# Relative values of a decoder's third self-attention: one product per query with its exps as the stationary operand

## The chip, the cores and the metric

The kernel runs on one core of one Trainium2 chip. The metric is the device time of one execution of the whole program, in microseconds (us); the kernel before was timed three times. TensorE (PE in the profile, PEld for its weight loads) multiplies, VectorE (DVE), ScalarE (ACT) and GpSimd (POOL) do the element-wise work, SyncE (SP) issues DMAs. A matrix product has a stationary operand, which is loaded into the array first (LDWEIGHTS), and a moving operand, which streams through it (MATMUL). In float32 the profile holds two LDWEIGHTS and two MATMUL records for each product, and one of each for a transpose.

## The reference

The model has four decoder layers of self-attention, cross-attention and feed-forward, twelve blocks in all, on x of shape (8, 128, 128). The change lies in the third layer's self-attention alone:

```python
def _L2_attn_ref(hidden_states, Wq, bq, Wk, bk, Wv, bv, Wo, bo, rel_k_emb, rel_v_emb):
    B, T, E = hidden_states.shape          # 8, 128, 128; H = 16 heads of D = 8
    ...                                    # qh, kh, vh: (B, H, T, D)
    score1 = jnp.einsum('bhqd,bhkd->bhqk', qh, kh)
    rel_k = _rel_embeds(rel_k_emb, T, T)   # table[q - k + 128], (T, T, D)
    s2 = jnp.einsum('bhqd,qkd->qbhk', qh, rel_k) ...
    attn = jax.nn.softmax((score1 + s2) / scaling, axis=-1)
    w1 = jnp.einsum('bhqk,bhkd->bhqd', attn, vh)
    rel_v = _rel_embeds(rel_v_emb, T, T)   # (q, k, d)
    se = attn.reshape(B * H, T, T).transpose(1, 0, 2)
    w2 = jnp.einsum('qnk,qkd->qnd', se, rel_v)      # the part that the change rewrites
    ...
    return (w1 + w2) ... @ Wo.T + bo
```

For w2 each query q has a matrix of its own, rel_v[q] (128 keys by 8), that is multiplied with the attention rows of all 128 pairs of a head and a batch.

## The kernel before

Each block is one function; the blocks run one after another with a barrier between them, and within a block each engine's instructions stand in program order and wait for each other by semaphores. `layer_l2_attn` first makes queries, keys and values, then the relative scores of the keys (L2446 to L2464), then runs sixteen pipelined steps of scores, exp, values and norm (L2473 to L2494). The exps of all heads and batches stay in `sm.prob`, 128 keys on the partitions by (16 heads times 8 batches) by 128 queries, so that the 128 exps of one query and one key lie 128 elements apart. The ordinary values, divided by the sum of exps, are in `sm.o`.

After the steps comes what the change touches:

- **Products** (L2496 to L2505). For every query, `relv[:, q, :]` (128 keys by 8 values and a column of ones) is stationary, 9 columns wide, and the query's exps move, 32 at a time in four products, each into its own group of 32 output partitions. That is 512 products. The results of 16 queries fill one PSUM bank; eight banks are filled.
- **Copies** (L2550 to L2554 on ACT, L2588 to L2592 on DVE). Each bank is copied to `oR` as it comes, ACT and DVE by turns. `oR` lies over `qm`, which is no longer needed.
- **Tail.** PE waits for the last copies (L2508 to L2510), then for each batch turns four 128x128 blocks back so that queries are on the partitions (L2512). DVE takes the reciprocal of the ones' column (L2598) and multiplies (L2603), POOL adds the result to `sm.o` (L2424), PE turns the sum (L540), ACT copies it out (L620), PE multiplies it with the output weights (L545), and DVE adds it to x (L596). A batch's turns, norm, sum, turn and projection are software-pipelined over the ten passes of `for step in range(B + 2)`; `part` has two halves, so the multiply of batch b waits for the sum of batch b - 2.

The next block is `layer_l2_xattn` (its first PE work is L664, L667 and the transposes L445). Three other places serve for comparison: L888 and L1143 are the routers' logits (tokens 128x128 stationary, 8 columns moving), L764 makes joined weights in the next layer's self-attention (128x128 stationary, 32 or 16 columns moving), and L3573 is a convolution whose stationary operand has 8 columns that lie 128 elements apart.

Of the kernel before, what the change touches and what calls it, by code (L numbers as in the profile page):

```python
# [12 lines left out]
ALU = mybir.AluOpType  # L13
# [11 lines left out]
P = 128  # L25

B = 8
# [7 lines left out]
BANK = 512  # L35
# [2345 lines left out]
def layer_l2_attn(core, tag, w):  # L2381

    nc, ps, norm = core.nc, core.ps, NormInBlock(core)
    c = Carve(core.scratch)
    wq, wk, wv, wo, of_four, bq, bk = w.take(P), w.take(P), w.take(P), w.take(D), w.take(4), w.take(4), w.take(1)
    bq1, bv, bo, relk, relv = w.take(1), w.take(D), w.take(D), w.take(2 * P), w.take(P, 9)
    qm = w.take(4, B * P)
    sm = RelativeHeads(core, c, wo, more=Carve(core.xnT), o=w.take(B * 16, 8))  # L2390
    oR = qm.rearrange("p i t -> p (i t)").rearrange("p (b j t) -> p b j t", b=B, j=4)
    part, part_inv = w.take(2 * 16, 8).rearrange("p (u h) d -> p u h d", u=2), w.take(2, 16)
    made_of = sm.prob.rearrange("p (b j i) q -> p j b i q", b=B, j=4)
    read_by = sm.prob.rearrange("p (y s m z) q -> p y z s m q", y=2, s=8, z=2)
    keys = core.xn[:, :, :].rearrange("p b d -> p (b d)")
    TURN = 16
    ROUNDS = P // TURN
# [8 lines left out]
    with nc.Block(tag, no_gpsimd_drain=True) as block:  # L2406

        @block.gpsimd
        def _(pool):
# [12 lines left out]
            for b in range(B):  # L2422
                pool.wait_ge(relv_normed.sem, relv_normed.at(b))
                nc.gpsimd.tensor_tensor(sm.o_of(b), sm.o_of(b), part[:, b % 2, :, :], ALU.add) \  # L2424
                    .then_inc(relv_summed.sem, relv_summed.up())

        @block.tensor
        def _(pe):
# [7 lines left out]
            for b in range(B):  # L2436
                v = nc.tensor.matmul(ps[2 + b // 4][:, b % 4 * P:(b % 4 + 1) * P], core.xnT[:, b * P:(b + 1) * P],
                                     wv, start=True, stop=True)
# [7 lines left out]
            for r in range(ROUNDS):  # L2446
# [8 lines left out]
                for t in range(TURN):  # L2455
                    q = r * TURN + t
# [16 lines left out]
            for p in range(-2, sm.STEPS + 2):  # L2473
# [11 lines left out]
                if p % 2 and p >= 3:  # L2485
                    b = (p - 3) // 2
# [9 lines left out]
            for r in range(ROUNDS):  # L2496
                if r == 7:
                    pe.wait_ge(sm.normed.sem, sm.normed.at(B - 1))
                for t in range(TURN):
                    q = r * TURN + t  # L2500
                    for i in range(4):
                        m = nc.tensor.matmul(
                            ps[r][32 * i:32 * i + 9, 32 * t:32 * t + 32].rearrange("p (b j) -> p b j", b=B),
                            relv[:, q, :], read_by[:, i % 2, i // 2, :, :, q], start=True, stop=True)
                m.then_inc(relv_made.sem, relv_made.up())  # L2505
            for step in range(B + 2):
                if step < B:
                    if step == 0:  # L2508
                        pe.wait_ge(relv_act.sem, relv_act.at(3))
                        pe.wait_ge(relv_dve.sem, relv_dve.at(3))  # L2510
                    for j in range(4):
                        t = nc.tensor.transpose(ps[step][:, j * P:(j + 1) * P], oR[:, step, j, :], core.ident[:, :])  # L2512
                    t.then_inc(relv_back.sem, relv_back.up())
                if 1 <= step <= B:
                    pe.wait_ge(relv_summed.sem, relv_summed.at(step - 1))
                    sm.pe_turn_out(pe, step - 1, step - 1)
                if step >= 2:
                    sm.pe_project(pe, step - 2, step - 2)

        @block.scalar  # L2520
        def _(act):
# [28 lines left out]
            for r in range(0, ROUNDS, 2):  # L2550
                act.wait_ge(relv_made.sem, relv_made.at(r))
                nc.scalar.copy(oR[:, :, :, r * TURN:(r + 1) * TURN],
                               ps[r][:, :].rearrange("p (t b j) -> p b j t", t=TURN, b=B)) \
                    .then_inc(relv_act.sem, relv_act.up())  # L2554
# [4 lines left out]
        def _(dve):  # L2559
# [28 lines left out]
            for r in range(1, ROUNDS, 2):  # L2588
                dve.wait_ge(relv_made.sem, relv_made.at(r))
                nc.vector.tensor_copy(oR[:, :, :, r * TURN:(r + 1) * TURN],  # L2590
                                      ps[r][:, :].rearrange("p (t b j) -> p b j t", t=TURN, b=B)) \
                    .then_inc(relv_dve.sem, relv_dve.up())  # L2592
            for step in range(B + 2):
                if step < B:
                    b = step
                    dve.wait_ge(relv_back.sem, relv_back.at(b))
                    o = ps[b][:, :].rearrange("p (h d) -> p h d", d=32)
                    nc.vector.reciprocal(part_inv[:, b % 2, :], o[:, :, 8]) \  # L2598
                        .then_inc(relv_inverse.sem, relv_inverse.up())
                    dve.wait_ge(relv_inverse.sem, relv_inverse.at(b))  # L2600
                    if b >= 2:
                        dve.wait_ge(relv_summed.sem, relv_summed.at(b - 2))
                    nc.vector.tensor_tensor(part[:, b % 2, :, :], o[:, :, 0:8],  # L2603
                                            part_inv[:, b % 2, :].unsqueeze(2).broadcast_to([P, 16, 8]), ALU.mult) \
                        .then_inc(relv_normed.sem, relv_normed.up())
                if step == 2:
                    dve.wait_ge(x_biased.sem, x_biased.at(0))
                if step >= 2:
                    sm.dve_add(dve, step - 2, step - 2)
# [1355 lines left out]
```

## Time and profile before

| | us |
|---|---|
| runs: median (lowest to highest of 3) | 1424.65 (1420.49 to 1427.03) |
| the profiled execution | 1414.56 |
| its span, first to last instruction | 1412.7 |
| PE busy | 1227.3 (87% of the span) |
| the changed block's products, start of the first to start of the last | 928.7 to 957.0 |
| the tail, to the next block's first instruction | to 969.1 |

The profiled execution lasts 1.9 us longer than its span and lies 10.1 us below the median of the three runs. A window row gives each engine's busy time in a stretch and PEclk, the granted TensorE clock: 1.00 is 2.4 GHz, 0.50 is 1.2 GHz.

### The profile page before, as it was taken

The page shows a single profiled execution, that of the slowest core. Times are in us where ns is not written, and L with a number is a line of the kernel's source. Part 1 is how long each engine was busy: PE and PEld are TensorE (multiplying, and loading weights), DVE is VectorE, ACT ScalarE, POOL GpSimd, SP SyncE. Part 2 cuts the span into 40 slices and gives each one's busy share as a digit, 9 for nine tenths or more (in the row PEclk, how much of TensorE's full clock was granted, in tenths as well). Part 3 has the DMA queues.
Part 4 walks back from the last instruction along what each step waited for, and adds up shares of the span by engine and source line. Part 5 has one row for each costly group of instructions (what it writes and reads, how often), then busy time and mean ns, then how long its engine had stood idle before and what let it go on. Part 6 is the DMA issues. An engine that isn't in the chain of part 4 may idle for free. (4 is left out here: it accounts for less than half of the span.)

```text
span 1412.7 us, 25671 instructions
## 1 busy us (share of the span) xinstructions
PE 1227.3 (87%) x10296; PEld 905.8 (64%) x10296; DVE 685.4 (49%) x2133; ACT 515.5 (36%) x1170; POOL 437.2 (31%) x519
## 2 busy tenths in 40 slices
PE   6999697999878756987898899998989999977897
PEld 5868585788623433664665697795657775565575
DVE  5555533444489154774674315626842125745312
ACT  5534242443356322454354212213433323433231
POOL 7969220000245326754672400003000001041404
PEclk9999798999956678999899658999989997989899
DMA  5000402321290000000000000000021100001312
GB/s 159 1 4 1 188 7 90 91 61 47 95 255 1 1 10 23 1 1 0 2 1 1 9 2 1 2 4 1 2 82 45 31 29 1 1 4 37 121 29 46
DMA packets 51639, 52.51 MB, mean 37 GB/s; under 512 B 19553, under 2 KB 42337, under 8 KB 50497
## 3 DMA queue, kind: packets, MB, share of 16 engines
q1 hardware_dynamic: 50496, 48.77, 11.0%
q0 software_dynamic: 1024, 2.10, 0.7%
q8 instruction: 83, 1.36, 0.4%
q14 instruction: 36, 0.29, 0.1%
HBM read 43.65 MB, written 7.21 MB: 36 GB/s over the span
## 5 line engine op out<-in xcount | busy, mean ns | idle before, releaser
L615 ACT ACTIVATE scratch<-bank 128x512 f32<-128x512 f32 x96 | 52.4, 594 | 88.9 <-PE bank L516 88.9
L574 DVE TENSOR_REDUCE scratch<-bank 128x4 f32<-128x512 f32 x96 | 63.2, 686 | 35.4 <-PE bank L2469 22.4
L439 POOL TENSOR_TENSOR ln_rstd<-ln_ve,ln_half 128x4 f32<-128x4 f32 x28 | 28.7, 1025 | 155.7 <-DVE ln_ve L418 155.5
L2721 POOL TENSOR_TENSOR scratch<-scratch 128x16 f32<-128x16 f32 x16 | 51.7, 3231 | 51.8 <-DVE scratch L3062 51.8
L1085 PEld LDWEIGHTS bank<-scratch 128*128 128x128 f32 x512 | 59.5, 192 | 7.2 <-issue 7.2
L1114 ACT ACTIVATE scratch<-bank 128x512 f32<-128x512 f32 x64 | 38.2, 597 | 67.4 <-PE bank L1075 67.4
L580 DVE TENSOR_TENSOR scratch<-bank,scratch 128x512 f32<-128x512 f32 x96 | 61.4, 681 | 0.0
L1133 DVE SCALAR_TENSOR_TENSOR x_res<-bank,scratch,x_res 128x128 f32<-128x128 f32 x64 | 18.0, 344 | 87.6 <-PE bank L1085 87.6
L1075 PE MATMUL bank<-xnT,scratch 128*128 128x512 f32 x128 | 59.6, 611 | 0.0
L1085 PE MATMUL bank<-scratch 128*128 128x128 f32 x512 | 59.6, 275 | 0.0
L516 PEld LDWEIGHTS bank<-ident,scratch 128*128 128x128 f32 x384 | 42.7, 143 | 23.7 <-DVE scratch L580 17.0
L516 PE MATMUL bank<-ident,scratch 128*128 128x128 f32 x384 | 53.6, 283 | 4.7 <-DVE scratch L580 4.7
L2459 PE MATMUL bank<-weights 32*128 32x32 f32 x1024 | 54.7, 395 | 2.5 <-DVE scratch L2573 2.5
L2459 PEld LDWEIGHTS bank<-weights 32*128 32x128 f32 x1024 | 54.6, 327 | 3.3 <-issue 3.3
L500 PE MATMUL bank<-scratch 32*128 32x512 f32 x192 | 54.0, 643 | 1.4 <-ACT scratch L2542 1.4
L1293 PE MATMUL bank<-scratch 128*128 128x128 f32 (+1 forms) x352 | 47.0, 291 | 9.0 <-issue 8.9
L1293 PEld LDWEIGHTS bank<-scratch 128*128 128x128 f32 (+1 forms) x352 | 45.0, 201 | 13.5 <-issue 12.5
L2750 PE MATMUL bank<-weights,xnT 128*128 128x512 f32 x64 | 39.5, 714 | 14.8 <-DVE scratch L3032 14.2
L2424 POOL TENSOR_TENSOR weights<-weights 128x128 f32<-128x128 f32 x8 | 3.7, 458 | 154.0 <-DVE weights L2603 154.0
L1887 POOL TENSOR_TENSOR x_res<-x_res,scratch 128x256 f32<-128x256 f32 x4 | 2.9, 726 | 143.6 <-ACT scratch L2031 143.6
L1358 ACT ACTIVATE scratch<-bank 128x512 f32<-128x512 f32 (+1 forms) x48 | 25.4, 544 | 57.8 <-remote 27.5
L3264 POOL TENSOR_TENSOR scratch<-scratch 128x1024 f32<-128x1024 f32 (+5 forms) x48 | 42.9, 895 | 3.8
(564 smaller groups left out, 3023.7 us busy)
## 6 DMA issues: line engine op xcount, KB each, us to landing
scratch<-conv_kernels SPq DMA_DIRECT2D x8, 1024.0 KB, 11.2
scratch<-e_l_ffn_w SPq DMA_DIRECT2D x20, 256.0 KB, 2.9
scratch<-e_l_ffn_w SPq DMA_DIRECT2D x4, 1024.0 KB, 14.8
values<-scratch SPq DMA_DIRECT2D x8, 512.0 KB, 2.6
scratch<-values SPq DMA_DIRECT2D x8, 512.0 KB, 4.3
weights<-w_l_ffn SPq DMA_DIRECT2D x1, 3698.0 KB, 11.6
scratch<-e_l_ffn_w SPq DMA_DIRECT2D x4, 768.0 KB, 9.5
weights<-w_l_attn SPq DMA_DIRECT2D x1, 2560.5 KB, 8.8
```

The costliest lines, as they stand in the source:

```text
L500: s = self.nc.tensor.matmul(self.by_head(self.core.ps[n % 4][:, :]), self.qT[rows, b * P:(b + 1) * P], self.km[rows, :, b * P:(b + 1) * P] ...
L516: t = self.nc.tensor.transpose(self.core.ps[4 + n % 2][:, i * P:(i + 1) * P], self.shift[:, n % 4, i * P:(i + 1) * P], self.core.ident[:, :])
L574: self.nc.vector.tensor_reduce(self.top[:, n % 4, :], self.by_head(self.core.ps[n % 4][:, :]), AX_X, ALU.max, negate=True).then_inc(self.t ...
L580: self.nc.vector.tensor_tensor(self.by_head(self.shift[:, n % 4, :]), self.by_head(self.core.ps[n % 4][:, :]), self.top[:, n % 4, :].unsqu ...
L615: self.nc.scalar.activation(self.prob_of(n), self.by_head(self.core.ps[4 + n % 2][:, :]), ACT.Exp, scale=scale) \
L1075: nc.tensor.matmul(ps[UP_BANKS[i]][:, :], wa[e % 2][:, i * P:(i + 1) * P], core.xnT[:, half(h)], start=True, stop=True).then_inc(up_made.s ...
L1085: mm = nc.tensor.matmul(ps[Y_BANKS[u % 3]][:, t * P:(t + 1) * P], hT[h][:, i, t * P:(t + 1) * P], wb[e % 2][:, i, :], start=(i == 0), stop ...
L1293: mm = nc.tensor.matmul(ps[Y_BANKS[j % 3]][0:n, t:t + P], hT[j % 2][:, i, t:t + n], wb[:, e, i, :], start=(i == 0), stop=(i == HC - 1))
L2459: m = nc.tensor.matmul(ps[4 * (r % 2) + j][:, 32 * t:32 * t + 32].rearrange("p (i b) -> p i b", i=4), relk[rows, P - 1 - q:2 * P - 1 - q], ...
L2721: nc.gpsimd.tensor_tensor(rn, ss, power, ALU.pow).then_inc(rooted.sem, rooted.up())
L2750: nc.tensor.matmul(ps[QK_BANKS[n]][:, :], core.xnT[:, b * P:(b + 1) * P], wqkv[d][:, n * BANK:(n + 1) * BANK], start=True, stop=True).then ...
L3264: link(tt(out, prod[:, :, 0:h], prod[:, :, h:2 * h], ALU.add))
```

## The change

The operands of the relative values swap their places: for each query all 128 exps become the stationary operand and `relv[:, q, :]` with its 9 columns moves. The result of a query is 9 columns wide with (head, batch) on all 128 partitions. 56 queries fit a bank, so three banks hold them (56, 56 and 16 queries), and three copies instead of eight put them into `oR`, now nine planes of 128 queries. Nine transposes bring back the plane of ones and the eight planes of values, for all batches at once; one reciprocal and four multiplies of 256 columns norm them; POOL adds batch by batch as before, now from strided views.

```diff
-    oR = qm.rearrange("p i t -> p (i t)").rearrange("p (b j t) -> p b j t", b=B, j=4)
-    part, part_inv = w.take(2 * 16, 8).rearrange("p (u h) d -> p u h d", u=2), w.take(2, 16)
+    over_queries = Carve(qm.rearrange("p i t -> p (i t)"))
+    oR, part, part_inv = over_queries.take(9, P), over_queries.take(8, 2, P // 2), over_queries.take(2, P // 2)
+    HELD = BANK // 9 // 2 * 2
+    HELDS = [slice(n, min(n + HELD, P)) for n in range(0, P, HELD)]
+    ONES_BANK, PART_BANKS = len(HELDS), (len(HELDS) + 1, len(HELDS) + 2)
+    held = lambda r: (oR[:, :, HELDS[r]].rearrange("p d q -> p q d"),
+                      ps[r][:, 0:9 * (HELDS[r].stop - HELDS[r].start)].rearrange("p (q d) -> p q d", d=9))
...
 (POOL)
-                pool.wait_ge(relv_normed.sem, relv_normed.at(b))
-                nc.gpsimd.tensor_tensor(sm.o_of(b), sm.o_of(b), part[:, b % 2, :, :], ALU.add) \
+                pool.wait_ge(relv_normed.sem, relv_normed.at(2 * (b // 4) + 1))
+                o = sm.o_of(b).rearrange("p (m y) d -> p d y m", y=2)
+                nc.gpsimd.tensor_tensor(o, o, part[:, :, :, 8 * b:8 * b + 8], ALU.add) \
...
 (PE)
-            for r in range(ROUNDS):
-                if r == 7:
-                    pe.wait_ge(sm.normed.sem, sm.normed.at(B - 1))
-                for t in range(TURN):
-                    q = r * TURN + t
-                    for i in range(4):
-                        m = nc.tensor.matmul(
-                            ps[r][32 * i:32 * i + 9, 32 * t:32 * t + 32].rearrange("p (b j) -> p b j", b=B),
-                            relv[:, q, :], read_by[:, i % 2, i // 2, :, :, q], start=True, stop=True)
+            for r, queries in enumerate(HELDS):
+                for q in range(queries.start, queries.stop):
+                    t = q - queries.start
+                    m = nc.tensor.matmul(ps[r][:, 9 * t:9 * t + 9], sm.prob[:, :, q], relv[:, q, :], start=True, stop=True)
                 m.then_inc(relv_made.sem, relv_made.up())
-            for step in range(B + 2):
+            pe.wait_ge(relv_dve.sem, relv_dve.at(0))
+            pe.wait_ge(relv_act.sem, relv_act.at(1))
+            nc.tensor.transpose(ps[ONES_BANK][:, 0:P], oR[:, 8, :], core.ident[:, :]) \
+                .then_inc(relv_back.sem, relv_back.up())
+            for n in range(2):
+                for d in range(4):
+                    t = nc.tensor.transpose(ps[PART_BANKS[n]][:, d * P:(d + 1) * P], oR[:, 4 * n + d, :], core.ident[:, :])
+                t.then_inc(relv_back.sem, relv_back.up())
+            for step in range(B + 1):
                 if step < B:
-                    if step == 0:
-                        pe.wait_ge(relv_act.sem, relv_act.at(3))
-                        pe.wait_ge(relv_dve.sem, relv_dve.at(3))
-                    for j in range(4):
-                        t = nc.tensor.transpose(ps[step][:, j * P:(j + 1) * P], oR[:, step, j, :], core.ident[:, :])
-                    t.then_inc(relv_back.sem, relv_back.up())
-                if 1 <= step <= B:
-                    pe.wait_ge(relv_summed.sem, relv_summed.at(step - 1))
-                    sm.pe_turn_out(pe, step - 1, step - 1)
-                if step >= 2:
-                    sm.pe_project(pe, step - 2, step - 2)
+                    pe.wait_ge(relv_summed.sem, relv_summed.at(step))
+                    sm.pe_turn_out(pe, step, step)
+                if step >= 1:
+                    sm.pe_project(pe, step - 1, step - 1)
...
 (ACT)
-            for r in range(0, ROUNDS, 2):
+            for r in (0, 2):
                 act.wait_ge(relv_made.sem, relv_made.at(r))
-                nc.scalar.copy(oR[:, :, :, r * TURN:(r + 1) * TURN],
...
+                nc.scalar.copy(*held(r)).then_inc(relv_act.sem, relv_act.up())
...
 (DVE)
+            dve.wait_ge(relv_made.sem, relv_made.at(1))
+            nc.vector.tensor_copy(*held(1)).then_inc(relv_dve.sem, relv_dve.up())
+            dve.wait_ge(relv_back.sem, relv_back.at(0))
+            nc.vector.reciprocal(part_inv, ps[ONES_BANK][:, 0:P].rearrange("p (y c) -> p y c", y=2)) \
+                .then_inc(relv_inverse.sem, relv_inverse.up())
+            dve.wait_ge(relv_inverse.sem, relv_inverse.at(0))
+            for h in range(2):
+                batches = slice(32 * h, 32 * h + 32)
+                for n in range(2):
+                    dve.wait_ge(relv_back.sem, relv_back.at(1 + n))
+                    nc.vector.tensor_tensor(
+                        part[:, 4 * n:4 * n + 4, :, batches],
+                        ps[PART_BANKS[n]][:, :].rearrange("p (d y c) -> p d y c", d=4, y=2)[:, :, :, batches],
+                        part_inv[:, :, batches].unsqueeze(1).broadcast_to([P, 4, 2, 32]), ALU.mult) \
+                        .then_inc(relv_normed.sem, relv_normed.up())
+            dve.wait_ge(x_biased.sem, x_biased.at(0))
+            for b in range(B):
+                sm.dve_add(dve, b, b)
```

On PE, from the end of the sixteen steps to the next block, there stood before (output by its name, operands, shape as output partitions by columns; `L540` is a batch's turn, `L545` its projection):

```order
L535 MATMUL bank<-ident,xnT 128x128 x4
L2502 MATMUL bank<-scratch,weights 9x32 x512
L2512 MATMUL bank<-ident,weights 128x128 x8
L540 MATMUL bank<-ident,weights 128x128
L2512 MATMUL bank<-ident,weights 128x128 x4
L540 MATMUL bank<-ident,weights 128x128
L545 MATMUL bank<-weights,xnT 128x128
L2512 MATMUL bank<-ident,weights 128x128 x4
L540 MATMUL bank<-ident,weights 128x128
L545 MATMUL bank<-weights,xnT 128x128
```

In the changed kernel (its line numbers are those of its own file) the same place reads:

```order
L535 MATMUL bank<-ident,xnT 128x128 x4
L2507 MATMUL bank<-weights,scratch 128x9 x128
L2511 MATMUL bank<-ident,weights 128x128
L2515 MATMUL bank<-ident,weights 128x128 x8
L540 MATMUL bank<-ident,weights 128x128 x2
L545 MATMUL bank<-weights,xnT 128x128
L540 MATMUL bank<-ident,weights 128x128
L545 MATMUL bank<-weights,xnT 128x128
```

The 512 products became 128 of another shape, and the turns back, which stood in fours between a batch's turn and projection, all stand ahead of the first batch.

On DVE, over the same stretch, there stood before (reciprocal, multiply, and from the third batch on the add to x):

```order
L2590 COPY weights<-bank 128x32x16 x4
L2598 RECIPROCAL weights<-bank 128x16
L2603 TENSOR_TENSOR weights<-bank,weights 128x128
L2598 RECIPROCAL weights<-bank 128x16
L2603 TENSOR_TENSOR weights<-bank,weights 128x128
L2598 RECIPROCAL weights<-bank 128x16
L2603 TENSOR_TENSOR weights<-bank,weights 128x128
L596 TENSOR_TENSOR x_res<-x_res,bank 128x128
```

Now the norm is done in five instructions before the first add:

```order
L2591 COPY weights<-bank 128x56x9
L2593 RECIPROCAL weights<-bank 128x128
L2600 TENSOR_TENSOR weights<-bank,weights 128x8x32 x4
L596 TENSOR_TENSOR x_res<-x_res,bank 128x128 x8
```

What moved is the norm: DVE's sixteen small instructions, spread over the batches, are five ahead of them.

## Rows read from the trace of the kernel before

**Rows 1.** The page: the span, and PE's and PEld's busy time.
```profile
span 1412.7 us, 25671 instructions
PE 1227.3 (87%) x10296; PEld 905.8 (64%) x10296; DVE 685.4 (49%) x2133; ACT 515.5 (36%) x1170; POOL 437.2 (31%) x519
```

**Rows 2.** Windows (start:end, length; PE, PEld, DVE, ACT, POOL busy; PEclk; DMA): products, tail.
```profile
928.70:957.20 28.50, 28.43 (x1025) 27.97 (x1024) 3.00 (x5) 2.35 (x4) 0.00 (x0) 1.00 0.02 5
957.20:969.10 11.90, 8.06 (x61) 6.23 (x56) 7.01 (x25) 2.13 (x8) 3.66 (x8) 1.00 0.00 0
```

**Rows 3.** One line's instructions, L888: count, ns min/median/max.
```profile
L888 PEld LDWEIGHTS bank<-weights,xnT x32: 286/333/333, 1039.6 to 1310.2; 128*128 128x128 f32 x32
L888 PE MATMUL bank<-weights,xnT x32: 351/361/361, 1039.6 to 1310.3; 128*128 128x8 f32 x32
```

**Rows 4.** Timeline of PE (start, duration us, operation, count): other stretches.
```profile
1039.60 3.55 PE L888 MATMUL bank<-weights,xnT 128*128 128x8 f32 x16 [0.88 <-DVE xnT L1122]
...
794.49 0.91 PE L2459 MATMUL bank<-weights 32*128 32x32 f32 x16 [2.51 <-DVE scratch L2573]
...
1159.04 3.20 PE L764 MATMUL bank<-weights 128*128 128x32 f32 x18 [1.56 <-PEq L1045]
...
1150.18 7.31 PE L1085 MATMUL bank<-scratch 128*128 128x128 f32 x64
...
852.61 3.73 PE L2469 MATMUL bank<-ident,scratch 128*128 128x128 f32 x16
857.33 2.05 PE L2469 MATMUL bank<-ident,scratch 128*128 128x128 f32 x16
```

**Rows 5.** Windows around L2459 and L764, columns as in rows 2.
```profile
794.50:794.90 0.40, 0.40 (x12) 0.40 (x13) 0.00 (x0) 0.40 (x1) 0.00 (x0) 0.78 0.00 0
794.90:848.00 53.10, 53.10 (x1003) 53.10 (x1001) 9.02 (x14) 8.22 (x16) 14.33 (x9) 0.50 0.01 2
850.60:856.00 5.40, 5.40 (x20) 3.90 (x20) 0.69 (x1) 0.00 (x0) 0.00 (x0) 0.50 0.00 0
1159.00:1159.90 0.90, 0.86 (x8) 0.89 (x9) 0.86 (x5) 0.90 (x1) 0.32 (x1) 1.00 0.00 0
1160.50:1168.20 7.70, 7.70 (x38) 7.70 (x38) 3.25 (x17) 0.74 (x2) 2.02 (x2) 0.50 0.14 52
```

**Rows 6.** Narrow weights, 128 elements apart (L3573) and side by side (L527).
```profile
L3573 PEld LDWEIGHTS bank<-scratch x256: 91/97/133, 480.3 to 493.2; 128*8 128x8 f32 x128
...
L527 PEld LDWEIGHTS bank<-scratch x768: 86/91/92, 867.0 to 1242.8; 128*9 128x9 f32 x192
```

**Rows 7.** Timeline of the tail.
```profile
957.33 0.69 DVE L2590 COPY weights<-bank 128x512 f32<-128x512 f32 x1 [6.48 <-PE bank L2502]
...
958.16 1.06 PE L2512 MATMUL bank<-ident,weights 128*128 128x128 f32 x8 [0.88 <-DVE weights L2590]
...
959.49 0.95 POOL L2424 TENSOR_TENSOR weights<-weights 128x128 f32<-128x128 f32 x2 [149.97 <-DVE weights L2603]
...
967.25 0.33 PE L540 MATMUL bank<-ident,weights 128*128 128x128 f32 x1 [0.30 <-POOL weights L2424]
...
968.46 0.29 DVE L596 TENSOR_TENSOR x_res<-x_res,bank 128x128 f32<-128x128 f32 x1 [0.33 <-PE bank L545]
```

**Rows 8.** Groups by line and form: busy us, mean ns, idle before.
```profile
L620 ACT COPY xnT<-bank 128x128 f32<-128x128 f32 x8 | 2.1, 266 | 11.6 <-PE bank L540 11.6
...
L3044 DVE TENSOR_TENSOR scratch<-bank,scratch 128x256 f32<-128x256 f32 x32 | 12.0, 416 | 0.0
...
L2424 POOL TENSOR_TENSOR weights<-weights 128x128 f32<-128x128 f32 x8 | 3.7, 458 | 154.0 <-DVE weights L2603 154.0
...
L1887 POOL TENSOR_TENSOR x_res<-x_res,scratch 128x256 f32<-128x256 f32 x4 | 2.9, 726 | 143.6 <-ACT scratch L2031 143.6
```

**Rows 9.** Timeline: the next block's first PE work.
```profile
969.14 1.95 PE L664 MATMUL bank<-ctxT_sb,weights 96*128 96x512 f32 x4 [0.72 <-PEq L2406]
...
970.93 1.95 PE L667 MATMUL bank<-weights,ctxT_sb 96*128 96x128 f32 x16
```

More of the change, by code:

```diff
@@ L2390, in layer_l2_attn @@
     sm = RelativeHeads(core, c, wo, more=Carve(core.xnT), o=w.take(B * 16, 8))
-    oR = qm.rearrange("p i t -> p (i t)").rearrange("p (b j t) -> p b j t", b=B, j=4)
-    part, part_inv = w.take(2 * 16, 8).rearrange("p (u h) d -> p u h d", u=2), w.take(2, 16)
+    over_queries = Carve(qm.rearrange("p i t -> p (i t)"))
[5 more added lines that the diff above has]
+                      ps[r][:, 0:9 * (HELDS[r].stop - HELDS[r].start)].rearrange("p (q d) -> p q d", d=9))
     made_of = sm.prob.rearrange("p (b j i) q -> p j b i q", b=B, j=4)
-    read_by = sm.prob.rearrange("p (y s m z) q -> p y z s m q", y=2, s=8, z=2)
     keys = core.xn[:, :, :].rearrange("p b d -> p (b d)")
@@ L2549, in _ @@
                     sm.act_outs(act, p // 2 - 1)
-            for r in range(0, ROUNDS, 2):
+            for r in (0, 2):
                 act.wait_ge(relv_made.sem, relv_made.at(r))
-                nc.scalar.copy(oR[:, :, :, r * TURN:(r + 1) * TURN],
-                               ps[r][:, :].rearrange("p (t b j) -> p b j t", t=TURN, b=B)) \
-                    .then_inc(relv_act.sem, relv_act.up())
+                nc.scalar.copy(*held(r)).then_inc(relv_act.sem, relv_act.up())
             for b in range(B):
@@ L2587, in _ @@
                     sm.dve_norm(dve, (p - 4) // 2, 7)
[L2588 to L2604, printed above, removed]
+            dve.wait_ge(relv_made.sem, relv_made.at(1))
@@ L2605, in _ @@
                         .then_inc(relv_normed.sem, relv_normed.up())
[L2606 to L2609, printed above, removed]
+            dve.wait_ge(x_biased.sem, x_biased.at(0))
+            for b in range(B):
+                sm.dve_add(dve, b, b)
 def layer_l1_ffn(core, tag, w):
```

## The prediction

> **What bounds the kernel now.** I read four views, in this order. The page says that PE is busy for 87% of the span [rows 1], so I expect a stage's time to be set on PE. A table by windows of the changed stretch confirms it: in the products' 28.5 us PE is busy for 28.43 at the high clock, with DVE busy for 3.0 and ACT for 2.35, so the copies hide completely; in the 11.9 us of the tail PE is busy for 8.06, DVE for 7.01 and POOL for 3.66, so there the chain from engine to engine sets the time and nobody is full [rows 2]. The products have 1024 records, so one costs 28.5 / 1024 = 27.8 ns. The third view is other lines whose operation looks like the new one, and the last is the granted clock around them. The reader should see that the question is not how many instructions there are, but what one of the new kind costs, and at which clock.
>
> **The products.** Removed: 512 products, 1024 records, 28.5 us. Added: 128 products, 256 records, each with a 128x128 weight load and 9 moving columns. That shape nearly stands in the trace: L888 loads 128x128 and moves 8 columns. Its 16 records take 3.55 us in all and one lasts 0.361 [rows 3, 4], so they start (3.55 - 0.36) / 15 = 0.213 us apart, at the 1.2 GHz clock. A matmul of 128 moving columns behind the same load runs at the high clock with 64 records in 7.31 us, (7.31 - 0.28) / 63 = 0.112 us apart [rows 4]. So the moving operand hardly matters and the weight load sets the pace: 0.213 us at the low clock, 0.107 to 0.112 at the high one. For 256 records that is 54.5 us or 27.3 to 28.6 us. At the high clock the change would win at most 1.2 us here, although it issues a quarter of the instructions, since each now loads 128 columns instead of 9.
>
> The granted clock then decides. Two stretches of the trace had a wide weight load for few moving columns and went on for long: L2459 (128 columns loaded, 32 moving) and L764 (128x128 loaded, 32 or 16 moving). Both began at the high clock, in both it fell to 1.2 GHz, and it stayed there for 53.1 us and 7.7 us, although PE shows busy for every one of those microseconds [rows 5]. Dense work brought it back only after about 5 us: at 0.50 from 850.6 to 856.0 [rows 5]. The new product moves 9 columns for 128 loaded, less than either, for 128 products in a row. I therefore take the low clock for the whole stage but its start. How long the start is: L2459 was reached after 2.51 us of idle and lost the clock 0.4 us later, L764 after 1.56 us and lost it after more than 0.9 us [rows 4, 5]. That is 2.9 and 2.5 us after the last dense record; I take 2.7 us, bounds 0 and 6. In 2.7 us at 0.107 come 25 records; the other 231 take 231 x 0.213 = 49.2 us. Stage: 51.9 us, and the last record ends 0.36 after its start where it was 0.27 or so, +0.1. **Products: 51.9 + 0.1 - 28.5 = +23.5 us**, bounds +20 and +26.
>
> Here two rules of the Trainium skill have a say. "TensorE: Matmul & The Clock Gate", section "What's actually happening", says that activity releases the throttle, the clock following how busy the engine has been. Read by the profile's busy share it would keep the clock high, and the sum would be that of the first rival. Rows 5 contradict that reading, since PE is 100% busy there at 1.2 GHz.
>
> The other is the note on cachelines in "SBUF — State Buffer", section "Door 1: The DMA port swizzle": each access that crosses to a new 16-byte line pays a penalty. By that rule the strided weight loads would be dearer than L888's contiguous ones, and the sum would be the second rival's. The trace agrees only to a small part, as the following shows.
>
> The new weights are read 128 elements apart. L3573 loads 8 such columns in 91/97/133 ns (min/median/max), L527 loads 9 adjacent ones in 86/91/92 [rows 6]. The medians differ by 6 ns over 8 columns; scaled to 128 it is 96 ns on a record, as an upper bound. The minima differ by 5 ns, which may as well be fixed. Bounds per record: 0 and +0.1 us at the high clock, so up to twice the price; I take 0, because at the low clock, where the stage will be, nothing of it shows: the full contiguous load of L888 lasts 333 ns and the slowest strided one of 8 columns 133, and (333 - 133) / 120 = 1.67 ns a column is just L888's own pace, 213 / 128 [rows 3, 6].
>
> **The copies.** Three in place of eight. Two of them finish under the products. The last holds 16 queries x 9 = 144 columns on ACT; the nearest row is 0.27 us for 128 columns [rows 8], so 0.28 for a copy of 0.69 that stood on the path [rows 7]. The gain is 0.4 us. A written stride of 128 elements has no row of its own; bounds 0.28 and 0.6.
>
> **The tail.** Before: the last product ends at about 957.3, the last add to x at 968.46 + 0.29 = 968.75 [rows 7], which is 11.45 us. I build the new one from T, the last product's end. The copy runs from T + 0.05 to T + 0.33; PE starts 0.14 later as before (957.33 + 0.69 to 958.16 [rows 7]), at T + 0.47. At the low clock transposes start (3.73 - 0.42) / 15 = 0.22 us apart, at the high one (2.05 - 0.27) / 15 = 0.12 [rows 4]. The clock is still low here. The fifth transpose ends at T + 0.47 + 4 x 0.22 + 0.42 = T + 1.8, the ninth at T + 2.65. The reciprocal hides under them; the multiplies of 256 columns cost 0.42 each [rows 8]; the first finishes at T + 2.2, the second at T + 3.1, and POOL starts at T + 3.2. Batches 0 to 3 need no more than these two; the other two multiplies (to T + 4.0) are ready before POOL reaches batch 4 at T + 5.1.
>
> POOL makes eight adds 0.475 us apart (0.95 for two [rows 7]), up to T + 7.0. Its views are strided now; for that I have no row, the nearest being 0.458 for the same 128 columns and 0.726 for twice as many [rows 8], so bounds of 0 and +2.1 us, and I take 0. PE needs for a batch a turn and two projection records, 3 x 0.22 = 0.65 us at the low clock and 0.36 at the high one. So at first PE sets the pace, and once the clock is back POOL does. Dense records of rows 5 needed 5 us for that, so about half of the eight batches run at either pace: 0.6 us more, T + 7.6. The last batch's turn, copy, projection and add took 968.75 - 967.25 = 1.5 us [rows 7]. End at T + 9.1, which is 2.3 us less than 11.45. **Tail: -2.3 us.** Bounds: all warm, T + 0.47 + 0.7 + 0.3 (five transposes, the rest of the ninth under the multiplies), POOL from T + 1.8, end at T + 7.1, which is -4.3; PE at its low pace throughout and POOL at its dear end, T + 11, which is -0.4. What is late next is POOL at the high clock and PE at the low one. The first batch's turn and projection, which started 2 us after T, now wait for the norm of all; that is in the sum.
>
> **The next block.** L664 and L667 take 3.7 us at the high clock [rows 9]. If the low clock reached them they would take up to 3.7 more. I think it comes back within the tail, which has 9 transposes and 24 further records; I take +1.0, bounds 0 and +3.7.
>
> **Sum.** 23.5 - 2.3 + 1.0 = +22.2 us. The rest of the program is the same instructions in the same order. Against the profiled execution of 1414.56 us (its span 1412.7 [rows 1] and 1.9 around it) this gives 1436.8. That execution is 10.1 us below the median of the runs, 1424.65, so for the measured time I add the difference to the median: 1424.65 + 22.2 = 1446.9, **1447 us**.
>
> **Rivals.**
>
> - *The clock stays at 2.4 GHz* (the other side). The stage starts from a long dense stretch instead of after idle time, which neither L2459 nor L764 did. Then the products cost 27.3 to 28.6 and save 0.6 on average, and the tail saves 4.3: -4.9 us, 1420. It decides from a clock that is high for over 25 us of the 27. Against it: the clock did not return in 53 us of L2459. Chance 0.06.
> - *The strided weight load costs double.* 512 cycles in place of 256, 0.427 us a record at the low clock: 231 x 0.213 = 49 us more, with a slightly shorter gain at the start, 1496. For it: the 6 ns of rows 6 and the page. Chance 0.06; milder forms of it (10% dearer, +5 us) belong to the range of the main case.
> - *The clock comes and goes* within the stage, low for half of it: products +11, tail -3, 1433. For it: in rows 5 the clock was high for the first 0.4 and 0.9 us of such work. Against: it never came back before dense work did. Chance 0.06.
>
> **Chances.** Forecast 0.82, its own range 1438 to 1457 (products ±3, tail ±2, next block -1 to +2.7, and the runs' own spread, 1420.5 to 1427). What a measurement can tell from no change is 0.5%, 7.1 us. The first rival lies inside it, mostly: faster 0.02, same 0.05 (with a little of the third). Everything else is slower: 0.93. Range 1436 to 1458: the three rivals and the edges of the forecast leave about 0.2 outside.
>
> **What would show it.** PEclk 0.5 in the window of the new products from their third microsecond on, weight loads of 0.333 us starting 0.213 apart, a stage of 52 us; transposes of the tail 0.22 apart; POOL's eight adds following each other with DVE already done. Wrong would be: a stage near 28 us at PEclk 1.0 (first rival); weight loads well over 0.333 us (second); PEclk between 0.6 and 0.9 over the stage (third); POOL adds over 0.6 us each would make the tail no shorter.

## The result, and the profile after

| | before | changed | ratio, 95% interval |
|---|---|---|---|
| median of the first comparison (4 runs each) | 1422.57 | 1450.20 | 1.0197 [1.0166, 1.0227] |
| median of a later one (16 and 5 runs) | 1422.06 | 1448.61 | 1.0188 [1.0164, 1.0212] |
| profiled execution | 1414.56 | 1449.16 | |

The changed kernel is slower by 27 us: 27.6 in the first comparison, 26.6 in the later one. The forecast of 1447 us lies 3 us from the measured 1450.20. As the experiments show, one of the reasons given for it was not what set the pace.

The products, read from the windows of the changed kernel's own product line (start:end, length, PE and PEld busy with records in the window, PEclk, DMA):

```profile
931.70:935.10 3.40, 3.40 (x17) 3.40 (x17) 1.00 0.00 0
935.20:986.90 51.70, 51.70 (x240) 51.70 (x239) 0.50 0.00 1
```

These answer to the first row of [rows 2]. The clock fell as forecast, 3.5 us into the stage, and stayed down. But the records tell something else: 17 in 3.40 us is one every 0.20 to 0.21 (one of them belongs to the window's edge), 240 in 51.7 is one every 0.215, and over the whole stage it is 55.3 / 255 = 0.217. **The pace is the same at both clocks.** The forecast's sum had 0.107 for the first part and 0.213 for the second. The line's own instructions (count, ns min/median/max, first and last start) say it in another way:

```profile
L2507 PEld LDWEIGHTS bank<-weights,scratch x256: 295/310/313, 931.6 to 986.9; 128*128 128x128 f32 x128
L2507 PE MATMUL bank<-weights,scratch x256: 281/366/371, 931.7 to 987.0; 128*128 128x9 f32 x128
```

A weight load lasts 295 to 313 ns throughout, in the first 3.4 us at the high clock as well as later. L888's, of the same size, adjacent and mostly at the low clock, lasts 333 [rows 3]. In a run told below, with adjacent weights and the clock high throughout, the same load lasts 190 to 192:

```profile
L2509 PEld LDWEIGHTS bank<-weights,scratch x256: 190/192/192, 928.5 to 957.0; 128*128 128x128 f32 x128
```

None of the changed kernel's loads is that short. The stage goes from 931.7 to 987.0 + 0.37 = 987.3, 55.7 us in place of 28.6.

The tail, as a timeline (start, duration, what it waited for), answers to [rows 7]:

```profile
987.37 0.40 ACT L2556 COPY weights<-bank 128x144 f32<-128x144 f32 x1 [30.25 <-PE bank L2507]
...
987.91 0.45 PE L2511 MATMUL bank<-ident,weights 128*128 128x128 f32 x1 [0.58 <-ACT weights L2556]
...
988.15 1.91 PE L2515 MATMUL bank<-ident,weights 128*128 128x128 f32 x8
988.40 0.96 DVE L2593 RECIPROCAL weights<-bank 128x128 f32<-128x128 f32 x1 [6.96 <-PE bank L2511]
989.39 0.42 DVE L2600 TENSOR_TENSOR weights<-bank,weights 128x256 f32<-128x256 f32 x1
990.10 1.09 DVE L2600 TENSOR_TENSOR weights<-bank,weights 128x256 f32<-128x256 f32 x3 [0.29 <-PE bank L2515]
990.61 4.08 POOL L2432 TENSOR_TENSOR weights<-weights 128x128 f32<-128x128 f32 x8 [177.94 <-DVE weights L2600]
...
991.21 0.98 PE L540 MATMUL bank<-ident,weights 128*128 128x128 f32 x2 [1.15 <-POOL weights L2432]
...
996.00 0.42 PE L540 MATMUL bank<-ident,weights 128*128 128x128 f32 x1
...
996.87 0.73 DVE L596 TENSOR_TENSOR x_res<-x_res,bank 128x128 f32<-128x128 f32 x2 [0.33 <-PE bank L545]
...
997.99 1.95 PE L664 MATMUL bank<-ctxT_sb,weights 96*128 96x512 f32 x4 [0.72 <-PEq L2413]
```

It ends at 997.6, 10.3 us after the products, where it was 11.45. POOL's eight adds take 4.08 us in a row and are done at 994.7. PE's eight turns, each followed by its projection, start 0.68 us apart (991.21 to 996.00), with the granted clock at 0.50 up to 996. So it is PE at the low clock that sets this part, and POOL is ahead of it. The next block starts with products of 1.95 us for four records, as in [rows 9]: the low clock did not reach it. From the start of the products to the next block's first product it is 66.3 us (931.68 to 997.99) where it was 40.5 (928.67 to 969.14): **+25.8 us**.

The two spans differ by 34.6. Some 3.0 us lie before the changed stage. They do not belong to the change: over all profiles of this case the stage starts between 923.7 and 934.3 us, and in the changed kernel's second profile it starts at 927.1, ahead of both profiles of the kernel before (928.7 and 929.5). The other 5.8 lie behind it, in the next block, which took 76.6 us up to the routers' products (998.0 to 1074.6) where it had taken 70.5; the rest of the program took 0.3 less. In the changed kernel the clock fell in it:

```profile
998.00:1010.30 12.30, 10.40 (x54) 5.88 (x56) 9.29 (x34) 5.92 (x12) 6.35 (x6) 1.00 0.01 0
1010.30:1023.90 13.60, 13.60 (x73) 7.12 (x70) 8.82 (x15) 3.76 (x7) 2.19 (x2) 0.50 0.00 1
```

PEclk is the third number from the end. The experiments tell whether that belongs to the change.

### The profile page after: what moved, and what is told of

It reads as the page before. It is cut to its first block and busy times, and to the rows that moved or that the text cites. A ratio compares the mean times of both kernels' runs of the same rounds, so it can differ in the third digit from the quotient of the medians.

```text
span 1447.3 us, 24068 instructions
## 1 busy us (share of the span) xinstructions
PE 1264.5 (87%) x9505; PEld 938.6 (65%) x9505; DVE 682.2 (47%) x2119; ACT 515.1 (36%) x1168; POOL 438.3 (30%) x519
## 3 DMA queue, kind: packets, MB, share of 16 engines
q1 hardware_dynamic: 50496, 48.77, 10.7%
## 5 line engine op out<-in xcount | busy, mean ns | idle before, releaser
L439 POOL TENSOR_TENSOR ln_rstd<-ln_ve,ln_half 128x4 f32<-128x4 f32 x28 | 28.7, 1026 | 162.8 <-DVE ln_ve L418 162.7
L2719 POOL TENSOR_TENSOR scratch<-scratch 128x16 f32<-128x16 f32 x16 | 51.7, 3232 | 50.9 <-DVE scratch L3060 50.9
L500 PE MATMUL bank<-scratch 32*128 32x512 f32 x192 | 57.3, 679 | 1.4 <-ACT scratch L2546 1.4
L2507 PEld LDWEIGHTS bank<-weights,scratch 128*128 128x128 f32 x256 | 55.7, 310 | 0.0
L2507 PE MATMUL bank<-weights,scratch 128*128 128x9 f32 x256 | 55.7, 366 | 0.0
```

The costliest lines, as they stand in the source:

```text
L500: s = self.nc.tensor.matmul(self.by_head(self.core.ps[n % 4][:, :]), self.qT[rows, b * P:(b + 1) * P], self.km[rows, :, b * P:(b + 1) * P] ...
L2507: m = nc.tensor.matmul(ps[r][:, 9 * t:9 * t + 9], sm.prob[:, :, q], relv[:, q, :], start=True, stop=True)
L2719: nc.gpsimd.tensor_tensor(rn, ss, power, ALU.pow).then_inc(rooted.sem, rooted.up())
```

## The experiments

Two theories stood against each other. **A:** a weight load whose elements lie 128 apart has a pace of its own, 0.217 us a record, whatever the clock. **B**, which the forecast's sum used: the pace is that of an adjacent load and only the granted clock matters. The first three runs and the changed kernel form a square: weights strided or adjacent, 9 or 128 columns moving.

### Adjacent weights, 9 columns moving

```diff
-  m = nc.tensor.matmul(ps[r][:, 9 * t:9 * t + 9], sm.prob[:, :, q], relv[:, q, :], start=True, stop=True)
+  m = nc.tensor.matmul(ps[r][:, 9 * t:9 * t + 9], sm.prob[:, q, :], relv[:, q, :], start=True, stop=True)
```

> The changed kernel, but each product's stationary operand is 128 adjacent elements of the exps (another query's set, so the values are not the reference's) instead of 128 elements that lie 128 apart. 9 columns move as in the changed kernel. Theory A (a strided weight load sets the pace, 0.217 us a record at either clock): as long as the clock is high, in the first 3 us or so, records start 0.107 us apart instead of 0.217; once it has fallen, 0.213. Stage 50 to 53 us, time about 3 us below the changed kernel. Theory B (only the granted clock sets the pace, as I predicted): 0.217 apart in the first microseconds too, stage 55.7 as in the changed kernel, no change.

Measured: 1444.85 us, ratio 1.0155 [1.0117, 1.0193]. Windows of the product line:

```profile
930.80:933.90 3.10, 3.10 (x29) 3.10 (x29) 1.00 0.00 0
934.00:982.00 48.00, 48.00 (x227) 48.00 (x227) 0.50 0.00 1
```

29 records in 3.10 us at the high clock, 0.107 to 0.112 each; 227 in 48.0 at the low one, 0.21 each. Stage 51.7 us, and the time is 4 to 5 us below the changed kernel's 1448.61 and 1450.20, where about 3 were expected. The forecast had 51.9 for the stage: its sum describes this kernel with adjacent weights, not the changed one. Theory A stands: with the stride gone the pace follows the clock.

### Strided weights, 128 columns moving

```diff
+  wide = min(P, 9 * (P - q))
-  m = nc.tensor.matmul(ps[r][:, 9 * t:9 * t + 9], sm.prob[:, :, q], relv[:, q, :], start=True, stop=True)
+  m = nc.tensor.matmul(ps[r][:, 9 * t:9 * t + wide], sm.prob[:, :, q], relv_flat[:, 9 * q:9 * q + wide], ...)
```

> The changed kernel with its strided weights, but 128 columns of the relative values move behind each load instead of 9; of the result only the 9 are kept (the next product writes over the rest). 40 queries fill a bank instead of 56, so there are four copies instead of three. I expect the granted clock to be 1.00 in the stage. Theory A (strided weights set the pace at either clock): records stay 0.217 us apart, stage 54 to 56 us, and only the tail and the next block gain, by 2 to 8 us in all. Theory B (the clock sets the pace): 0.11 us apart, stage about 28 us, time 25 to 32 us below the changed kernel.

Measured: 1448.98 us, ratio 1.0184 [1.0146, 1.0221].

```profile
933.80:987.90 54.10, 54.10 (x248) 54.10 (x248) 1.00 0.00 1
```

The clock is at 2.4 GHz for 54 us, and a record still takes 54.1 / 248 = 0.218. Theory B falls. The 2 to 8 us expected from tail and next block did not come: in the profiled run, the slowest of its four (1453.75 us), the clock fell at the last, narrower products, PEclk was 0.59 on average in the tail, and from the products' end to the next block it took 10.3 us, where the changed kernel took 10.7.

### Adjacent weights, 128 columns moving

Both edits together.

> Both edits together: the weights are 128 adjacent elements (another query's set, so the values are not the reference's) and 128 columns move. Both theories expect the high clock and records 0.107 to 0.115 us apart, a stage of 27 to 30 us and a time within 0.5% of the kernel before. If the stage stays near 55 us, neither the stride nor the clock is what costs.

Measured: 1419.45 us, ratio 0.9988 [0.9961, 1.0016], no difference from the kernel before.

```profile
928.70:957.00 28.30, 28.30 (x255) 28.30 (x255) 1.00 0.00 1
```

28.3 / 255 = 0.111 us a record. Only with both costs gone does the stage return to 28.6 us. In a table, us a record and us a stage:

| | 9 columns move | 128 columns move |
|---|---|---|
| weights 128 apart | 0.217, 55.7 (changed kernel; clock low) | 0.218, 56.1 (clock high) |
| weights adjacent | 0.213, 51.7 (clock low) | 0.111, 28.7 (clock high) |

Each cause alone costs nearly everything; together they cost hardly more. They do not add: the strided load has its 0.217 at either clock, and the adjacent load at the low clock happens to have almost the same pace, 0.213. The tail of this run, 957.3 to the next block at 966.8, takes 9.5 us with the clock partly high, 2.4 less than before.

### How far apart may weights lie

The kernel with 128 moving columns, whose weights lie 2 elements apart for the first 40 queries, then 4, then 3, and 128 for the last 8:

```diff
+  HELD, STEPS_OF = 40, (2, 4, 3, 128)
-  ... sm.prob[:, :, q], ...
+  ... sm.prob.rearrange("p n q -> p (n q)")[:, q:q + (P - 1) * STEPS_OF[r] + 1:STEPS_OF[r]], ...
```

> As the kernel with 128 moving columns (clock high), but the 128 weights of a product lie 2 elements apart for the first 40 queries, 4 apart for the next 40, 3 apart for the next 40 and 128 apart for the last 8 (other exps than the reference's, so the values are not the reference's). Theory A1 (what costs is that each 16-byte line is used for one element only): 0.112 us a record for 2 apart, 0.217 for 4 and for 128, and in between or 0.217 for 3. Theory A2 (any step but 1 costs): 0.217 in all four parts. Theory A3 (only large steps cost): 0.112 for 2, 3 and 4, 0.217 for 128.

One run, 1433.57 us. One window inside each part:

```profile
924.00:933.00 9.00, 9.00 (x78) 9.00 (x77) 1.00 0.01 2
934.00:951.00 17.00, 17.00 (x75) 17.00 (x74) 1.00 0.00 0
953.00:965.00 12.00, 12.00 (x71) 12.00 (x70) 1.00 0.00 1
967.00:969.20 2.20, 2.20 (x12) 2.20 (x11) 1.00 0.00 0
```

With a record less for the edges: 0.117 to 0.119 us for 2 apart, 0.23 for 4, 0.17 for 3, 0.20 to 0.22 for 128. Counted in groups of four fp32 elements (16 bytes, called lines here), 128 elements at these steps touch 64, 128, 96 and 128 of them. The times follow that count: 0.23 / 128 = 1.8 ns a line for a record, times 96 it is 0.17, and times 64 it is 0.117. That is theory A1; any step costing the same (A2) and only large steps costing (A3) both fall. What A1 leaves open is that 4 apart (0.23) is some 6% dearer than 128 apart (0.217) at the same number of lines.

The Trainium skill ("SBUF — State Buffer", section "Door 1: The DMA port swizzle") says that the memory has 16-byte lines and gives full speed with two hits to a line. The trace agrees nearly: 0.118 for two hits to a line, against 0.111 for adjacent elements, and 0.23 for one hit. So at the high clock one hit to a line costs a factor of two over an adjacent fp32 load, and at the low clock nothing visible (0.217 against 0.213).

### What had set the pace before

```diff
-  relv[:, q, :], read_by[:, i % 2, i // 2, :, :, q], start=True, stop=True)
+  relv[:, q, :], sm.prob[:, q, 32 * i:32 * i + 32].rearrange("p (b j) -> p b j", b=B), start=True, stop=True)
```

> The kernel before, but the 32 exps that move in each of its products are adjacent elements (another query's set, so the values are not the reference's) instead of 128 apart. If strided reads set the pace of the old products too (27.8 ns a record for 32 columns in four groups of output partitions that can run side by side), the stage shortens clearly, to 10 to 20 us from 28.5. If it was the pace at which instructions start, it stays at 26 to 28.5 us.

Measured: 1424.47 us, ratio 1.0017 [0.9994, 1.0039]; stage 28.9 us. The stage did not get shorter, so the second answer, the pace at which instructions start, is the nearer one. The timeline of PE shows that the work itself did get shorter:

```profile
933.24 1.26 PE L2502 MATMUL bank<-scratch,weights 128*9 128x32 f32 x128 [2.63 <-issue]
937.26 1.89 PE L2502 MATMUL bank<-scratch,weights 128*9 128x32 f32 x128 [2.75 <-issue]
941.00 1.89 PE L2502 MATMUL bank<-scratch,weights 128*9 128x32 f32 x128 [1.85 <-issue]
```

128 records run in 1.3 to 1.9 us, and then PE waits 1.9 to 2.8 us for nothing that this view shows, over and over, 4.0 us a round: about 31 ns for a record with its weight load. The clock is not the reason. It fell to 0.50 in this run after the first of the three rounds shown, which made the work longer (1.26 to 1.89 us), and the round stayed about as long (4.0, then 3.7 and 4.0). The DMA view of the same trace shows what goes in step with the rounds: from 928 to 958 us the only traffic is seven packets of 16 KB of the queue `q8 instruction`, 4.0 us apart. So the supply of PE's instructions is the likely limit. Two runs with half the instructions followed, 64 columns to a product:

```diff
-  for i in range(4):
-      ... ps[r][32 * i:32 * i + 9, 32 * t:32 * t + 32] ..., read_by[:, i % 2, i // 2, :, :, q]
+  for i in range(2):
+      g, u = 2 * (t % 2) + i, t // 2
+      ... ps[r][32 * g:32 * g + 9, 64 * u:64 * u + 64], sm.prob[:, 64 * i:64 * i + 64, q]   # or [:, q, 64 * i:...]
```

> The kernel before with half as many products, each of 64 strided moving columns instead of 32, written to the four groups of output partitions by turns (the results are put in other places, so the values are not the reference's). As many exps are read as before, by half the instructions. Theory C (the supply of PE's instructions sets the old pace, about 4 us for 128 records in the run with adjacent columns): 512 records take 15 to 18 us. Theory D (reading strided columns sets it, 64 reads in 27.8 ns): the stage stays at 27 to 29 us.

> As the run with half as many products of 64 columns, but the columns are adjacent (other exps than the reference's, results in other places). Theory C (instruction supply): 15 to 18 us, as with the strided columns. Theory D: less than the strided one, 7 to 17 us. If it takes clearly less than half of the 28.9 us of the full number of products, instruction supply isn't the bound.

Strided: 1421.89 us, ratio 1.0001 [0.9967, 1.0034]. Adjacent: 1410.12 us in its one run. The strided stage, without a gap, and two rounds of the adjacent one:

```profile
931.64 26.68 PE L2503 MATMUL bank<-scratch,weights 128*9 128x64 f32 x512
```
```profile
934.99 1.97 PE L2503 MATMUL bank<-scratch,weights 128*9 128x64 f32 x128 [1.42 <-issue]
938.46 1.97 PE L2503 MATMUL bank<-scratch,weights 128*9 128x64 f32 x128 [1.50 <-issue]
```

The old stage had two limits that happened to agree. Reading: half the instructions with the same strided columns still take 26.7 us (theory D), 52 ns for the 64 columns of a record, 0.81 ns each, about half the 217 / 128 = 1.7 ns of a strided weight. Instructions: with adjacent columns a round of 128 records takes 3.5 us (64 columns) or 4.0 us (32 columns), 27 to 31 ns a record; why it is not the same in both is not known. The adjacent half version's stage came out at 12.3 us, below theory C's 15 to 18 and also less than half of 28.9, which the expectation had named as a sign against the supply of instructions. The timelines answer that: in both runs the first 209 records came without a wait, and only the remaining 303, there 815, had to wait in every round.

### Pairs of queries

Both limits point to the same edit of the kernel before: read two neighbouring queries at once, 8 bytes of a line instead of 4, with half the products.

```diff
-  for t in range(TURN):
+  for t in range(0, TURN, 2):
...
-      ps[r][32 * i:32 * i + 9, 32 * t:32 * t + 32] ...,
-      relv[:, q, :], read_by[:, i % 2, i // 2, :, :, q], start=True, stop=True)
+      ps[r][32 * i:32 * i + 18, 32 * t:32 * t + 64].rearrange("p (n e) -> p n e", e=2),
+      relv[:, q:q + 2, :].rearrange("p q d -> p (q d)"), read_by[:, i % 2, i // 2, :, q:q + 2], ...)
...
+  parity: 1 in column e where the query's number is e modulo 2; the reciprocals are multiplied with it
+  (POOL) o += part[b % 2][:, :, 0, :];  o += part[b % 2][:, :, 1, :]
```

> A version built on the kernel before: two neighbouring queries share a product. Stationary are both queries' relative values, 18 columns; the exps move in pairs (q, q + 1), which are 8 bytes wide, 64 columns to a product; 256 products in place of 512. Half of the result is not wanted (a query's exps with its neighbour's values) and is weighted with 0 when the sums are divided; DVE has one small instruction and POOL one add more per batch. It computes the reference. Theory A1 (a 16-byte line costs about the same whether one or two of its elements are used, on the moving side too): half as many lines are read, the stage takes 14 to 17 us instead of 28.6, the tail 1 to 3 us more, and the time falls by 9 to 13 us, ratio 0.991 to 0.994. Rival (the moving side pays for each element): as many elements as before, the stage stays at 26 to 28 us and the time rises by 0 to 3 us.

Measured: 1414.99 us (median of 11 runs) against 1422.06, ratio **0.9946 [0.9927, 0.9966]**, faster than both kernels, by 7 us where 9 to 13 were expected. The profile is that of its slowest run, 1421.06 us, whose mean granted clock (0.878) is also the lowest of the eleven (up to 0.891). The windows of stage and tail (all engines, PEclk third from the end):

```profile
934.30:948.20 13.90, 13.84 (x513) 13.53 (x512) 3.37 (x8) 3.02 (x8) 0.00 (x0) 1.00 0.02 5
...
952.00:958.00 6.00, 5.28 (x23) 4.53 (x24) 3.14 (x11) 1.06 (x4) 2.74 (x6) 0.50 0.00 0
958.00:967.40 9.40, 6.75 (x27) 4.92 (x26) 4.83 (x16) 1.08 (x5) 3.73 (x9) 0.50 0.00 0
```

The stage fell from 28.6 to 13.9 us, just below the 14 to 17 expected, so the rival is refuted: the moving side does not pay for each element. A record takes 27 ns, as in the rounds of the adjacent half version. No wait shows in it, though, and half of the strided reading would give 26, so this run does not tell the two limits apart.

The tail was a miss: expected 1 to 3 us more, it grew from 11.8 to 19.3 (948.1 to 967.4) in this profile. The clock fell early in it, but that is the smaller part. Two batches go through DVE, POOL and PE in a cycle, first here and then in the kernel before:

```profile
953.34 0.36 DVE L2606 RECIPROCAL weights<-bank 128x32 f32<-128x32 f32 x1 [1.45 <-PE bank L2520]
...
954.47 0.46 POOL L2428 TENSOR_TENSOR weights<-weights 128x128 f32<-128x128 f32 x1 [1.50 <-DVE weights L2613]
...
955.52 0.48 PE L540 MATMUL bank<-ident,weights 128*128 128x128 f32 x1 [0.72 <-POOL weights L2431]
...
957.32 0.36 DVE L2606 RECIPROCAL weights<-bank 128x32 f32<-128x32 f32 x1 [0.57 <-PE bank L2520]
```
```profile
960.81 0.26 DVE L2598 RECIPROCAL weights<-bank 128x16 f32<-128x16 f32 x1 [0.91 <-PE bank L2512]
...
961.47 0.45 POOL L2424 TENSOR_TENSOR weights<-weights 128x128 f32<-128x128 f32 x1 [1.03 <-DVE weights L2603]
...
961.98 0.33 PE L540 MATMUL bank<-ident,weights 128*128 128x128 f32 x1 [0.36 <-POOL weights L2424]
```

The cycle takes 3.98 us where it took 2.20, up to the reciprocal at 963.01. Of the 1.78 more, DVE's wider and additional instructions take 0.47 (1.13 against 0.66), POOL's second add 0.54 (1.05 against 0.51) and PE at the low clock 0.77 (1.80 against 1.03). Four cycles make 7.1 of the 7.5 us: about 4 come from the added instructions, which the expectation had put at 1 to 3 although nothing hides them in this chain, and about 3 from the clock. In this profiled run half of the stage's gain was given back in the tail. The other ten runs were faster and have no profile; whether the clock can be kept was not tried.

### The next block's clock

> The kernel before, unchanged, for a second profile. The next block (first product of L664 to first routers' product of L888) took 70.5 us in the first profile and 75.0 to 79.7 in the changed kernel and four of its variants. If that difference is by chance of the granted clock and not of the change, this profile may show 75 us or more there, with a stretch of PEclk 0.5; if the change causes it, 70.5 again.

> The changed kernel, unchanged, for a second profile and more timed runs on the same chip as the pairs. Stage 55.5 to 56 us with records 0.217 apart at either clock, tail 10 to 10.5 us, ratio to the kernel before 1.017 to 1.022. The next block (first product of L664 to the first routers' product of L888) took 76.6 us in the first profile; if its fall of the clock belongs to the change, 75 us or more again, if it is chance it may be 70.5.

In the changed kernel's second profile the stage took 55.7 us, a record every 0.217 us, although the clock fell 2.8 us after its start instead of 3.5, and the tail 10.0 us, all as expected. In the next block the kernel before took 70.4 us again (970.0 to 1040.4), the changed one 75.0 (993.2 to 1068.2). That alone would speak for the change as the cause. But the run with half the strided products has the tail of the kernel before and a stage nearly as long, both at PEclk 1.00, and still took 76.6 us in the next block:

```profile
931.70:958.20 26.50, 26.50 (x513) 25.55 (x512) 3.03 (x5) 2.35 (x4) 0.00 (x0) 1.00 0.01 2
958.30:970.20 11.90, 7.98 (x57) 6.24 (x57) 7.02 (x25) 2.16 (x9) 3.71 (x9) 1.00 0.00 0
970.20:1046.80 76.60, 68.33 (x577) 40.40 (x577) 56.22 (x143) 29.91 (x60) 10.63 (x9) 0.87 0.08 26
```

So a fall that costs 6 us there needs neither the changed shape nor a low clock ahead of it. Still, the count is one-sided: the next block took 75.0 to 79.7 us in all ten profiles of other kernels, and 70.5 and 70.4 in the two of the kernel before. Both of these (1414.56 and 1415.87 us) lie low among its runs, whose medians are 1422, so they may be executions in which the clock happened to stay up. Its runs' mean granted clocks point that way: 0.897 and 0.895 in its two fastest of the last comparison (1414.17 and 1414.90 us, the profiles have 0.895 and 0.896), 0.883 to 0.889 in the four above 1425. The median difference, 27 us, is then the 25.8 of stage and tail and little else. In which block the slower runs lose the clock was not seen, since they have no profile; this stays likely, not shown.

## Why the forecast's number was right and one of its reasons wrong

- **The products, +23.5 us: the step that failed.** The prediction took "the weight load sets the pace: 0.213 us at the low clock, 0.107 to 0.112 at the high one", and set the surcharge of the stride to 0. Measured: +27.0 us, 0.217 a record at both clocks; the surcharge at the high clock is 0.217 - 0.111 = 0.106 us, not 0. The stride alone is enough (0.218 at the high clock). The low clock came as forecast but cost nothing in this stage; taken away alone it changes nothing (1.0184 against 1.0188). The sum was close by luck: the other, unneeded cause has the same price.
- **Where the reading went wrong.** The row was there: 97 against 91 ns in [rows 6]. Scaled to 128 columns it gave 96 ns, "up to twice the price", which is what the high clock showed (0.107 to 0.217). It was set to 0 on the ground that at the low clock nothing showed, which was also right. The rival "strided weight load costs double", 1496 us, was wrong in the other direction: it put the double price on top of the low clock, and the two do not multiply.
- **The start at the high clock**, 2.7 us forecast, was 3.5, and 2.8 in the second profile. In this kernel it brought nothing, where the sum had given it 25 records at 0.107; that is 2.7 of the 3.5 us by which the products were short.
- **The first rival's premise**, that a high clock would bring the time to 1420, fell with the run of 128 moving columns: clock high, 1449 us.
- **The tail, -2.3 us**: measured 10.3 in place of 11.45, -1.2. Up to POOL's start the forecast held: T + 3.2, measured 990.61 - 987.33 = 3.3. The last copy took 0.40 for 0.28, and the reciprocal of 128 columns (0.96 us) held the first multiply until 989.39, but POOL waited for the second, which waited for the ninth transpose at T + 2.7 as forecast. POOL's adds took 0.54 each, inside the bounds of 0.46 and 0.73, and were not what was late. The lost 1.2 us lie behind them: the forecast let half of the eight batches run at PE's high pace, and the clock stayed at 0.50 up to the eighth, so that the last turn started at T + 8.7 in place of T + 7.6.
- **The next block, +1.0 us**: nothing was carried over at its start; its later fall of the clock is told above.
- **The sum**: stage and tail came out at +25.8 us where the forecast had +21.2, or +22.2 with its term for the next block, and the medians differ by 27.6. The forecast's time lies only 3 us off because it was added to 1424.65, the median of the first three runs; on the 1422.57 of the comparison it would have been 1444.8, 5.4 off.
- **Range and chances**: 1450.2 lies in 1436 to 1458, and slower was right.

## What to carry to other kernels

When an operand moves from the moving side to the stationary one, its stride moves with it. Count the 16-byte lines that a weight load touches: in this case 128 fp32 weights on 128 lines cost 0.217 to 0.23 us a record (0.217 at either clock), on 64 lines 0.118. Two causes that bound the same stage are told apart only by taking each away alone and then both; a forecast that comes out right has not shown which of them it was.

## What the runs showed of the hardware that was not expected

- Records with an fp32 weight load of 128 columns start 0.107 to 0.112 us apart with adjacent columns at 2.4 GHz, 0.213 at 1.2 GHz, and 0.217 with columns 128 elements apart at both.
- Strided moving columns in four groups of output partitions cost 0.81 ns each in a record, strided weights 1.7.
- Two adjacent moving elements out of a line cost hardly more than one: 64 columns in pairs took 27 ns a record, singly 52.
- In the two runs with adjacent small products PE got through one fp32 record with its load in 27 to 31 ns once the first 209 records were done; the profile shows it as idle time "issue" after every 128 records, and 16 KB packets of the instruction queue in step with it. The link between the two is inferred.
- A DVE reciprocal grows with its width: 0.26 us for 16 columns, 0.96 for 128, where the multiply of 256 columns takes 0.42.
